# Node loop of a graph network kernel: the hidden product takes x by columns, the norm's factor goes behind it

## The chip, the cores and the metric

The kernel runs on one core of a Trainium2 chip. The metric is the device time of one execution in microseconds; beside it each profiled execution has a span, from its first to its last instruction. PE is TensorE, DVE VectorE, ACT ScalarE, POOL GpSimd, and SP the engine that issues the plain transfers.

## The reference

10,000 nodes of 512 numbers (`x`), 2,500 edges with 128 attributes each. Everything is float32.

```
h   = layernorm(x)                                   # no gain, no shift
m   = relu([h[src], attr] @ W1.T + b1) @ W2.T + b2   # per edge
agg = segment_sum(m, dst)
gi  = agg @ W_ih.T + b_ih ;  gh = h @ W_hh.T + b_hh  # 3 x 512 columns each
r, z = sigmoid(i_r + h_r), sigmoid(i_z + h_z)
n   = tanh(i_n + r * h_n)
h_new = (1 - z) * n + z * h
x1  = x + h + gamma * (h_new - run_mean) / sqrt(run_var + eps) + beta
h2  = layernorm(x1)
y   = x1 + 2 of 8 experts (512 -> 32 -> 512, chosen by a gate) of h2 + half a shared expert of h2
```

## The kernel before

Every fp32 product is made of three fp32r products: each operand is split into a high part (a rounding copy) and a low part (the rest), and hi*hi, hi*lo and lo*hi are added up in PSUM. A product of a tile of 128 rows by 512 x 512 is therefore twelve matmuls.

**Edges.** The 2,560 edges (padded) go in five super-groups of four tiles. For each the sources are gathered, normalised, turned on PE, sent through both layers, summed by destination, and multiplied by W_ih; the result, 3 x 512 columns per edge tile, is stored in a table in DRAM (`gates_in`). PE is busy nearly all of this time. In the last super-group the products with W_ih stand alone (`product`, L1146), while W_hh is loaded in four blocks of 128 x 1536 (L593, L604), ACT rounds them (`whh_hi`, L720) and DVE takes the rest (`whh_lo`, L815).

**Nodes.** Then follows a loop over 79 tiles of 128 nodes (`periods`, four tiles per loop step, the first and last ones written out). Each engine has its own body, in order, and the bodies meet through semaphores. `p.has(k)` marks what belongs to the tile k ahead of the current one. Per tile t:

- SP loads `xt` of tile t+2 (L1195) and stores the output of tile t-3 (L1185).
- DVE makes the first norm's mean and variance of tile t+2 (`first_norm`, L469, L454, L461, L462); POOL makes from it 1/sqrt (`rstd`, L1220), `shift` (L1223) and `one_rstd` (L1226).
- ACT makes `h` and `x_h` = x + h of tile t+1 (`first_rows`, L478, L481), POOL adds the batch norm's shift (`x_h_b`, L1264) and gathers the row of the edge table (`gates`, L1212).
- PE turns `h` of tile t+1 by four transposes (`turn_h`, L493), ACT rounds it from PSUM (`h_hi`, L1308), DVE takes the rest (`h_low`, L488).
- PE multiplies `h` of tile t by the three thirds of W_hh: r, n, then z (`gate`, L1455, twelve matmuls each). The z product is cut into two halves: ahead of the first comes `turn_h`, between them the transposes of `h2` of tile t-1.
- DVE adds the gates to r and z (`r_pre` L1438, `z_pre` L1384), ACT copies the n product (`hn_raw`, L1293), POOL adds the bias (`hn`, L1237), multiplies by r (`r_hn`, L1242), adds the gates (`n_pre`, L1246); ACT makes the tanh (`n_gate`, L1321), POOL h - n (`h_n`, L1251); five DVE instructions end in `x1` (L1403 to L1413).
- The second norm goes DVE, POOL (L1220, L1223), ACT (`h2`, L1298), PE (transposes), ACT (`h2_hi`, L1312), DVE (`h2_lo`, L1371), PE (twelve products with the experts' first layer, L1492).
- DVE makes `hid` (L1344 to L1365), PE turns it, ACT and DVE split it (`hid_hi` L1316, `hid_lo` L1375), PE multiplies (L1502, L1504), DVE adds `x1` into `y` (L1443).

ACT's order in a body is: `h`, `x_h`, `hn_raw`, `h2`, `r_gate`, `h_hi`, `h2_hi`, `hid_hi`, `n_gate`, `z_gate`, the experts' weights. POOL's is: second norm, `hn`, `r_hn`, `n_pre`, `h_n`, first norm, gather, `x_h_b`. DVE's is: `hid`, `first_norm`, `h2_lo`, `hid_lo`, `h_lo`, `z_pre`, the choice of experts, `x1` and its statistics, `r_pre`, `y`.

Before tile 0, DVE also splits the experts' weights (L1418 to L1431), ahead of `r_pre` of tile 0.

## Time and profile before

| what | value |
|---|---|
| three runs | 1437.27, 1438.11, 1442.31 us, median 1438.11 |
| profiled execution | 1442.45 us, of which span 1440.6 us |
| mean granted clock of TensorE | 0.989 |
| PE busy | 1378.2 us, 96% |
| PE weight loads (beside the matmuls) | 1136.4 us, 79% |
| DVE busy | 1098.6 us, 76% |
| ACT busy | 606.5 us, 42% |
| POOL busy | 900.3 us, 62% |
| memory traffic | 154.94 MB, mean 108 GB/s |

The profiled execution is 1.85 us longer than its span. A busy time counts the instructions of an engine that last; an engine that waits for a semaphore is idle. Matmuls overlap each other, and their ends are modelled, so the starts of consecutive matmuls say more than their durations. Lines such as L1455 are lines of the kernel before; helpers such as L493 serve several places, and the tile names tell them apart.

### The profile page before, as it was taken

The numbers are of one execution on the slowest core, as the hardware profiler recorded it, in microseconds if no ns is written. First come the engines' busy times: TensorE is split into PE (matmuls) and PEld (weight loads), VectorE is DVE, ScalarE is ACT, GpSimd is POOL, SyncE is SP. The second block draws the span as 40 slices with busy tenths as digits, with TensorE's granted clock in tenths as the row PEclk, the third lists the DMA queues.
The fourth block names the chain that finished last, engine by engine and source line by source line (L and its number), as shares of the span: only waits on it lengthen the run. The fifth ranks groups of instructions, "written<-read, shape, count | busy, mean of one in ns | idle before, by whom it ended". The sixth has DMA issues, their size and how long they took to land. (4 is left out here: it accounts for less than half of the span.)

```text
span 1440.6 us, 22894 instructions
## 1 busy us (share of the span) xinstructions
PE 1378.2 (96%) x6714; PEld 1136.4 (79%) x6714; DVE 1098.6 (76%) x2746; ACT 606.5 (42%) x1088; POOL 900.3 (62%) x1037
## 2 busy tenths in 40 slices
PE   4899999999899999999999999999999999999996
PEld 3678888787678888888888888888888888888884
DVE  3586334234588988888888888888888888888885
ACT  3431212202244444445444544454445444544441
POOL 3210142102387788878887788778887788778871
PEclk9999999999999999999999999999999999999997
DMA  8211432246323223322332233223322332333220
GB/s 306 68 68 64 161 129 103 88 144 223 142 95 110 99 83 109 109 92 90 109 109 89 93 109 109 84 98 109 109 81 101 109 108 76 107 109 104 79 94 30
DMA packets 50625, 154.94 MB, mean 108 GB/s; under 512 B 7840, under 2 KB 8480, under 8 KB 50464
## 3 DMA queue, kind: packets, MB, share of 16 engines
q0 software_dynamic: 15920, 79.97, 16.3%
q1 hardware_dynamic: 34672, 74.55, 14.3%
q8 instruction: 18, 0.29, 0.1%
q14 instruction: 15, 0.12, 0.0%
HBM read 117.22 MB, written 37.28 MB: 107 GB/s over the span
## 5 line engine op out<-in xcount | busy, mean ns | idle before, releaser
L1455 PE MATMUL bank<-whh_hi,h_hi 128*128 128x512 f32 x948 | 384.4, 406 | 7.0 <-DVE h_lo L488 7.0
L1455 PE MATMUL bank<-whh_hi,h_lo 128*128 128x512 f32 x948 | 373.3, 394 | 0.0
L1455 PE MATMUL bank<-whh_lo,h_hi 128*128 128x512 f32 x948 | 371.3, 392 | 0.0
L1455 PEld LDWEIGHTS bank<-whh_hi,h_hi 128*128 128x128 f32 x948 | 178.6, 188 | 41.1 <-DVE h_lo L488 7.4
L1455 PEld LDWEIGHTS bank<-whh_hi,h_lo 128*128 128x128 f32 x948 | 178.1, 188 | 39.0
L1455 PEld LDWEIGHTS bank<-whh_lo,h_hi 128*128 128x128 f32 x948 | 179.0, 189 | 34.1
L1212 POOL DMA_INDIRECT gates<-gates_in,slot_at x79 | 119.1, 1507 | 64.7 <-POOL slot_at L1210 63.3
L1293 ACT ACTIVATE hn_raw<-bank 128x512 f32<-128x512 f32 x79 | 47.2, 597 | 259.9 <-PE bank L1455 259.9
L1251 POOL TENSOR_TENSOR h_n<-h,n_gate 128x512 f32<-128x512 f32 x79 | 102.5, 1297 | 58.7 <-ACT n_gate L1321 58.7
L1237 POOL TENSOR_TENSOR hn<-hn_raw,hn_bias 128x512 f32<-128x512 f32 x79 | 104.0, 1317 | 45.5 <-ACT hn_raw L1293 45.5
L1264 POOL TENSOR_TENSOR x_h_b<-x_h,bn_shift 128x512 f32<-128x512 f32 x79 | 103.4, 1309 | 20.9 <-ACT x_h L481 18.4
L1492 PE MATMUL bank<-f_hi,h_hi 128*128 128x296 f32 x316 | 103.3, 327 | 11.3 <-DVE h_lo L1371 8.7
L1242 POOL TENSOR_TENSOR r_hn<-r_gate,hn 128x512 f32<-128x512 f32 x79 | 102.6, 1299 | 15.1 <-ACT r_gate L1303 4.1
L1246 POOL TENSOR_TENSOR n_pre<-r_hn,gates 128x512 f32<-128x512 f32 x79 | 101.0, 1279 | 12.4 <-POOL r_hn L1242 7.1
L493 PE MATMUL bank<-ident,h 128*128 128x128 f32 x632 | 95.2, 273 | 9.3 <-ACT h L1298 9.2
L493 PEld LDWEIGHTS bank<-ident,h 128*128 128x128 f32 x632 | 78.5, 141 | 31.2 <-ACT h L1298 11.0
L1146 PE MATMUL bank<-wih_hi,a_hi 128*128 128x512 f32 x240 | 95.5, 398 | 4.6 <-DVE wih_lo L815 2.5
L1220 POOL TENSOR_TENSOR rstd<-var_eps,minus_half 128x1 f32<-128x1 f32 x158 | 91.6, 580 | 9.1 <-DVE var_eps L462 9.1
L1492 PE MATMUL bank<-f_lo,h_hi 128*128 128x296 f32 x316 | 95.2, 301 | 0.0
L1492 PE MATMUL bank<-f_hi,h_lo 128*128 128x296 f32 x316 | 95.1, 301 | 0.0
L478 ACT ACTIVATE h<-xt,shift,rstd 128x512 f32<-128x512 f32 x79 | 64.5, 817 | 70.8 <-POOL one_rstd L1226 70.8
L1146 PE MATMUL bank<-wih_hi,a_lo 128*128 128x512 f32 x240 | 94.1, 392 | 0.0
(176 smaller groups left out, 3179.3 us busy)
## 6 DMA issues: line engine op xcount, KB each, us to landing
xt<-in_x SPq DMA_DIRECT2D x79, 256.0 KB, 3.1
out<-y SPq DMA_DIRECT2D x79, 256.0 KB, 3.0
gates_in<-g_out SPq DMA_DIRECT2D x16, 768.0 KB, 3.3
wih_lo_raw<-in_wih_t SPq DMA_DIRECT2D x4, 768.0 KB, 16.1
whh_lo_raw<-in_whh_t SPq DMA_DIRECT2D x4, 768.0 KB, 7.6
gates_in<-late_out SPq DMA_DIRECT2D x6, 256.0 KB, 5.7
gates_in<-g_out SPq DMA_DIRECT2D x6, 256.0 KB, 2.0
m_lo_raw<-in_attr_t SPq DMA_DIRECT2D x5, 256.0 KB, 2.7
```

What stands on the lines that cost most here:

```text
L478: act.activation(h[:, s, :], xt[:, s, :], ACT.Identity, bias=shift[1][:, s:s + 1], scale=rstd[1][:, s:s + 1]).then_inc(h_done, 1)
L493: last = pe.transpose(to[:, k * R:(k + 1) * R], rows_of[:, k * P:(k + 1) * P], ident[0:R, 0:R])
L1146: last = pe.matmul(to[0:R, :], a[:, k, j * R:(j + 1) * R], w[:, k, q * D:(q + 1) * D], start=n == 0, stop=n == 3 * DK - 1)
L1212: pool.indirect_dma_start(out=gates[:, s, :], out_offset=None, in_=gates_in, in_offset=bass.IndirectOffsetOnAxis(ap=slot_at[:, s:s + 1], a ...
L1220: pool.tensor_tensor(rstd[which][:, s:s + 1], var_eps[which][:, :], minus_half[0:R, 0:1], ALU.pow)\
L1237: pool.tensor_tensor(hn[:, s, :], hn_raw[:, s, :], hn_bias[:, :], ALU.add).then_inc(hn_done, 1)
L1242: pool.tensor_tensor(r_hn[:, :], r_gate[:, :], hn[:, s, :], ALU.mult).then_inc(r_hn_done, 1)
L1246: pool.tensor_tensor(n_pre[:, :], r_hn[:, :], gates[:, s, 2 * D:G3], ALU.add).then_inc(n_pre_done, 1)
L1251: pool.tensor_tensor(h_n[:, :], h[:, s, :], n_gate[:, s, :], ALU.subtract).then_inc(h_n_done, 1)
L1264: pool.tensor_tensor(x_h_b[:, s, :], x_h[:, s, :], bn_shift[:, :], ALU.add).then_inc(x_h_b_done, 1)
L1455: last = pe.matmul(to[0:R, :], a[:, s, k * R:(k + 1) * R], w[:, k, q * D:(q + 1) * D], start=n == 0, stop=n == 3 * DK - 1)
L1492: last = pe.matmul(b_f1[0:R, 0:F1], a[:, k * R:(k + 1) * R], w[:, k, :], start=n == 0, stop=n == 3 * DK - 1)
```

## The change

A second input is added, `x_cols`: for each node tile the same numbers of x, arranged by the host with the 512 features on the partitions. The product takes x instead of h. As h = rstd * (x - mean), and the mean of a row times the column sums of W_hh is what x @ W has too much, the rows of W_hh are centred on the chip: from each of the 1,536 rows its mean over the 512 inputs is subtracted, which makes the product of x equal to that of x - mean. The factor rstd multiplies the product where it leaves PSUM.

- Gone: the four transposes of `h` per tile, `h_hi`, `h_lo` and one PSUM bank's use for them. The bank serves as a second one for the r product, so that the wait for `r_pre` is one tile looser.
- Per tile new: SP's load of 256 KB of `x_cols` into the memory of `x_lo`, behind a wait for the z product; ACT's `x_high`, DVE's `x_low`, now from SBUF.
- `r_pre` and `z_pre` become scalar_tensor_tensor with `rstd`, `hn_raw` becomes an Identity with a scale.
- `first_norm` moves from DVE (four instructions) to ACT (four other ones), behind `x_h` and ahead of `hn_raw`.
- During the edges: four loads of three rows per partition of W_hh, twelve ACT instructions that sum them, a store of the means and their broadcast (768 KB); after the edges' last gathers POOL subtracts them in four instructions of 128 x 1536, and ACT's rounding waits for it.
- The experts' split on DVE moves from ahead of `r_pre` of tile 0 to behind its `z_pre`, two of its six steps are merged away; ACT's part of it moves behind `r_gate`.

```diff
-    def first_norm(dve, p):
-        s = p.slot(2)
-        dve.wait_ge(x_in[s], 16 * (p.turn(2) + 1))
-        dve.bn_stats(st[1][:, :], xt[:, s, :]).then_inc(st_done[1], 1)
-        statistics(dve, p, 2, 1)
-        mean_var(dve, p, 2, 1)
+    ROOT = math.sqrt(D)
+    def first_norm(act, p):
+        t, s = p.t, p.slot(2)
+        act.wait_ge(x_in[s], 16 * (p.turn(2) + 1))
+        wait_from(act, shift_done[1], 2 * (t + 2))
+        act.activation(squares[:, :], xt[:, s, :], ACT.Copy, scale=-1.0 / D, accum_out=neg_mean[1][:, :])\
+            .then_inc(mv_done[1], 1)
+        act.wait_ge(mv_done[1], t + 3)
+        act.activation(root_mean[:, :], neg_mean[1][:, :], ACT.Copy, scale=1.0 / ROOT).then_inc(root_done, 1)
+        act.wait_ge(root_done, t + 3)
+        act.activation(squares[:, :], xt[:, s, :], ACT.Square, bias=root_mean[:, :], scale=1.0 / ROOT,
+                       accum_out=var1[:, :]).then_inc(st_done[1], 1)
+        act.wait_ge(st_done[1], t + 3)
+        act.activation(var_eps[1][:, :], var1[:, :], ACT.Identity, bias=eps_col[:, :]).then_inc(var_done[1], 1)
...
-    def h_low(dve, p):
+    def x_high(act, p):
         s = p.slot(1)
-        dve.wait_ge(h_hi_done, p.t + 2)
-        dve.tensor_tensor(h_lo[:, s, :], b_th[:, 0:DK * R], h_hi[:, s, :].bitcast(F32), ALU.subtract)\
-            .then_inc(h_lo_done, 1)
+        act.wait_ge(cols_in[s], 16 * (p.turn(1) + 1))
+        wait_from(act, z_prod, p.t)
+        act.activation(x_hi[:, s, :], x_raw[:, s, :], ACT.Copy).then_inc(x_hi_done, 1)
+
+    def x_low(dve, p):
+        s = p.slot(1)
+        dve.wait_ge(x_hi_done, p.t + 2)
+        dve.tensor_tensor(x_lo[:, s, :], x_raw[:, s, :], x_hi[:, s, :].bitcast(F32), ALU.subtract)\
+            .then_inc(x_lo_done, 1)
...
@@ after the carries of the last super-group, POOL
+            pool.wait_ge(mean_back, 16)
+            for k in range(DK):
+                pool.wait_ge(whh_in[k], 16)
+                pool.tensor_tensor(whh_raw[:, k, :], whh_raw[:, k, :], whh_mean[:, :], ALU.subtract)\
+                    .then_inc(whh_centred, 1)
...
+            def sums_of_whh(n):
+                act.wait_ge(rows_in, 16 * (n + 1))
+                for i in range(3):
+                    at = 3 * n + i
+                    act.activation(whh_rows[:, i, :], whh_rows[:, i, :], ACT.Copy, scale=1.0 / D,
+                                   accum_out=mean_cols[:, at:at + 1]).then_inc(rows_summed, 1)
...
@@ ACT ahead of the node loop
             for k in range(DK):
+                if k == 0:
+                    first_norm(act, Period(0, -FIRST - 2))
                 if k == 2:
-                    first_rows(act, Period(0, -FIRST - 1))
-                act.wait_ge(whh_in[k], 16)
+                    first_norm(act, Period(0, -FIRST - 1))
+                    for j in range(2):
+                        x_high(act, Period(0, j - FIRST - 1))
+                act.wait_ge(whh_centred, k + 1)
                 hi_of(whh_hi[:, k, :], whh_raw[:, k, :]).then_inc(whh_hi_done, 1)
+            first_rows(act, Period(0, -FIRST - 1))
...
@@ SP's body of the node loop
                 if p.has(-3):
                     store(t - 3, p.slot(-3))
+                if p.has(2) and not p.early(2):
+                    wait_from(sp, z_prod, t + 1)
+                    sp.dma_start(x_raw[:, s, :], x_cols[bass.ds(at, 1), :, :].rearrange("o p r -> p (o r)"))\
+                        .then_inc(cols_in[s], 16)
...
@@ ACT's body
+                if p.has(2) and not p.early(2):
+                    first_norm(act, p)
                 if p.has(0):
                     act.wait_ge(n_prod, t + 1)
                     wait_from(act, hn_done, t - 1)
-                    act.activation(hn_raw[:, s, :], b_n[0:R, :], ACT.Copy).then_inc(hn_raw_done, 1)
+                    act.wait_ge(rstd_done[1], t + 1)
+                    act.activation(hn_raw[:, s, :], b_n[0:R, :], ACT.Identity,
+                                   scale=rstd[1][:, p.slot4(0):p.slot4(0) + 1]).then_inc(hn_raw_done, 1)
...
-                if p.has(1):
-                    act.wait_ge(h_turned, t + 2)
-                    wait_from(act, z_prod, t)
-                    act.activation(h_hi[:, s, :], b_th[:, 0:DK * R], ACT.Copy).then_inc(h_hi_done, 1)
+                if p.has(1) and not p.early(1):
+                    x_high(act, p)
...
@@ DVE's body
-                if p.has(2) and not p.early(2):
-                    first_norm(dve, p)
...
-                if p.has(1) and not p.first(1):
-                    h_low(dve, p)
+                if p.has(1) and not p.early(1):
+                    x_low(dve, p)
...
-                    dve.tensor_tensor(z_pre[:, :], b_z[0:R, :], gates[:, s, D:2 * D], ALU.add)
+                    dve.scalar_tensor_tensor(z_pre[:, :], b_z[0:R, :], rstd[1][:, p.slot4(0):p.slot4(0) + 1],
+                                             gates[:, s, D:2 * D], ALU.mult, ALU.add)
+                if p.first(0):
+                    split_of_experts(dve)
...
@@ PE's body
-                    pe.wait_ge(h_lo_done, t + 1)
-                    wait_from(pe, r_pre_done, t)
-                    gate(s, b_r, 0).then_inc(r_prod, 1)
+                    pe.wait_ge(x_lo_done, t + 1)
+                    wait_from(pe, r_pre_done, t - 1)
+                    gate(s, b_r[s], 0).then_inc(r_prod, 1)
                     wait_from(pe, hn_raw_done, t)
                     gate(s, b_n, 2).then_inc(n_prod, 1)
-                if p.has(1) and not p.first(1):
-                    turn_h(pe, p)
```

## Rows read from the trace of the kernel before

**Rows 1.** Windows: stretch, length, busy time of each engine, clock, DMA share, GB/s.
```profile
423.31:1395.84 972.53, 962.24 (x4886) 799.55 (x4885) 862.27 (x2296) 475.70 (x888) 778.19 (x889) 1.00 0.29 100
```
**Rows 2.** Timeline of ACT: start, duration, instruction, [idle before, what ended it].
```profile
423.31 0.60 ACT L1293 ACTIVATE hn_raw<-bank 128x512 f32<-128x512 f32 x1 [3.06 <-PE bank L1455]
...
1395.84 0.60 ACT L1293 ACTIVATE hn_raw<-bank 128x512 f32<-128x512 f32 x1 [3.18 <-PE bank L1455]
```
**Rows 3.** Timeline of PE in the tile at 900 us, and the next.
```profile
900.65 0.41 PE L1492 MATMUL bank<-f_hi,h_hi 128*128 128x296 f32 x1
...
909.47 0.60 PE L493 MATMUL bank<-ident,h 128*128 128x128 f32 x4
909.83 0.48 PE L1455 MATMUL bank<-whh_hi,h_hi 128*128 128x512 f32 x1
910.14 0.40 PE L1455 MATMUL bank<-whh_lo,h_hi 128*128 128x512 f32 x1
...
911.30 0.60 PE L493 MATMUL bank<-ident,h 128*128 128x128 f32 x4
...
913.13 0.49 PE L493 MATMUL bank<-ident,hid 128*128 128x128 f32 x3
```
**Rows 4.** Groups by line, weight loads, 423.31 to 1395.84: busy, mean ns, idle before.
```profile
L1492 PEld LDWEIGHTS bank<-f_hi,h_hi 128*128 128x128 f32 x296 | 55.7, 188 | 27.8 <-DVE h_lo L1371 27.8
```
**Rows 5.** Groups by line, POOL, the same stretch.
```profile
L1237 POOL TENSOR_TENSOR hn<-hn_raw,hn_bias 128x512 f32<-128x512 f32 x74 | 96.8, 1308 | 42.4 <-ACT hn_raw L1293 42.4
```
**Rows 6.** Timeline of ACT in the tile at 909 us.
```profile
909.75 0.60 ACT L1293 ACTIVATE hn_raw<-bank 128x512 f32<-128x512 f32 x1 [3.32 <-PE bank L1455]
910.24 0.81 ACT L1298 ACTIVATE h<-x,shift,rstd 128x512 f32<-128x512 f32 x1
...
911.95 0.59 ACT L1312 ACTIVATE h_hi<-bank 128x512 fp32r<-128x512 f32 x1
```
**Rows 7.** Groups by line and shape, ACT, the whole span.
```profile
L743 ACT ACTIVATE r_lo_raw<-bank,b_col 128x512 f32<-128x512 f32 x20 | 13.7, 687 | 39.6 <-PE bank L1098 39.6
L720 ACT ACTIVATE r_hi<-r_lo_raw 128x512 fp32r<-128x512 f32 x20 | 12.6, 632 | 0.6
...
L1303 ACT ACT_TABLE_LOAD x1 | 1.3, 1283 | 0.0
```
**Rows 8.** Timelines of POOL and PE in the tile at 410 us.
```profile
410.75 0.40 POOL L1223 TENSOR_TENSOR shift<-neg_mean,rstd 128x1 f32<-128x1 f32 x1
...
412.05 0.65 PE L493 MATMUL bank<-ident,h 128*128 128x128 f32 x4 [1.17 <-ACT h L1298]
```
**Rows 9.** Timelines of POOL and DVE, tiles at 425, 900 and 910 us.
```profile
425.56 0.20 DVE L1365 TENSOR_TENSOR hid<-extra,hid 128x41 f32<-128x41 f32 x1
...
900.26 1.28 POOL L1246 TENSOR_TENSOR n_pre<-r_hn,gates 128x512 f32<-128x512 f32 x1 [0.17 <-POOL r_hn L1242]
901.14 0.42 DVE L1375 TENSOR_TENSOR hid_lo<-bank,hid_hi 128x256 fp32r<-128x256 f32 x1 [0.54 <-ACT hid_hi L1316]
902.28 1.30 POOL L1251 TENSOR_TENSOR h_n<-h,n_gate 128x512 f32<-128x512 f32 x1 [0.74 <-ACT n_gate L1321]
...
910.51 1.36 POOL L1237 TENSOR_TENSOR hn<-hn_raw,hn_bias 128x512 f32<-128x512 f32 x1 [0.65 <-ACT hn_raw L1293]
910.75 1.18 DVE L1365 TENSOR_TENSOR hid<-extra,hid 128x41 f32<-128x41 f32 x1
```
**Rows 10.** Timelines of ACT, DVE and PE between edges and nodes.
```profile
355.68 1.49 ACT L720 ACTIVATE whh_hi<-whh_lo_raw 128x1536 fp32r<-128x1536 f32 x1 [0.39 <-DMA whh_lo_raw<-in_whh_t]
...
373.11 0.39 PE L1455 MATMUL bank<-whh_hi,h_hi 128*128 128x512 f32 x1
...
386.29 0.68 DVE L1438 TENSOR_TENSOR r_pre<-bank,gates 128x512 f32<-128x512 f32 x1
...
399.40 0.66 PE L493 MATMUL bank<-ident,h 128*128 128x128 f32 x4 [1.61 <-ACT h L1298]
```
**Rows 11.** The page, DMA issues: transfer, queue, count, size, median us to landing.
```profile
xt<-in_x SPq DMA_DIRECT2D x79, 256.0 KB, 3.1
```

More of the change, by code:

```diff
@@ L86, in gnn_ffn @@
     iota8 = place("iota8", [R, NE])
+    eps_col = place("eps_col", [R, 1])
     node_slot = place("node_slot", [R, NT], I32)
@@ L302, in gnn_ffn @@
     x_h_b = place("x_h_b", [R, 2, D])
[L303 to L306 removed]
+    x_hi = place("x_hi", [P, 2, DK * R], F32R)
+    x_lo, x_raw = place_low("x_lo", [P, 2, DK * R])
+    st = {2: place("st2", [R, 6])}
+    mv = {2: place("mv2", [R, 2])}
     var_eps = {k: place(f"var_eps{k}", [R, 1]) for k in (1, 2)}
     neg_mean = {k: place(f"neg_mean{k}", [R, 1]) for k in (1, 2)}
[L309 removed]
+    squares = place("squares", [R, D])
+    root_mean = place("root_mean", [R, 1])
+    var1 = place("var1", [R, 1])
+    rstd = {1: place("rstd1", [R, UNROLL]), 2: place("rstd2", [R, 2])}
     shift = {k: place(f"shift{k}", [R, 2]) for k in (1, 2)}
@@ L574, in _ @@
                 for j in range(1, SUP):
+                    if j == 2 and g > 1:
+                        rows_of_whh(2 * g - 3)
                     store(SUP * (g - 1) + j)
+                if g == 1:
+                    sp.wait_ge(bias_stored, 16)
+                if g < NSUP - 2:
+                    rows_of_whh(2 * g - 2)
                 if g == 2:
@@ L593, in _ @@
                 sp.dma_start(whh_raw[:, k, :], whhv[:, k, :]).then_inc(whh_in[k], 16)
+            for t in range(2):
+                sp.dma_start(x_raw[:, t, :], x_cols[t, :, :]).then_inc(cols_in[t], 16)
             for j in range(2, SUP):
@@ L1059, in _ @@
             last = EC - SUP
-            for k in range(2):
-                whh_lo_of(k)
-            for j in range(2):
-                for q in range(3):
-                    take_gates(last + j, q)
-            take_gates(last + 2, 0)
-            whh_lo_of(2)
-            take_gates(last + 2, 1)
-            whh_lo_of(3)
-            take_gates(last + 2, 2)
-            h_low(dve, Period(0, -FIRST - 1))
+            for q in range(3):
+                take_gates(last, q)
+            for q in range(3):
+                take_gates(last + 1, q)
+                if q < 2:
+                    whh_lo_of(q)
+            for j in range(2):
+                x_low(dve, Period(0, j - FIRST - 1))
+            for q in range(3):
+                take_gates(last + 2, q)
+                if q > 0:
+                    whh_lo_of(q + 1)
             for q in range(3):
@@ L1172, in _ @@
                 sums(g)
-            for j in range(SUP - 1):
+            for j in range(SUP):
                 product(NSUP - 1, j)
-            turn_h(pe, Period(0, -FIRST - 1))
-            product(NSUP - 1, SUP - 1)
             pe.wait_ge(g_added, 3 * EC - 3)
@@ L1453, in gate @@
                 for k in range(k0, k1):
-                    for a, w in ((h_hi, whh_hi), (h_hi, whh_lo), (h_lo, whh_hi)):
+                    for a, w in ((x_hi, whh_hi), (x_hi, whh_lo), (x_lo, whh_hi)):
                         last = pe.matmul(to[0:R, :], a[:, s, k * R:(k + 1) * R], w[:, k, q * D:(q + 1) * D],
```

118 lines of the change are left out of this document (67 added, 51 removed).

## Prediction

> **What bounds the kernel now.** I read the windows first: of a span of 1440.6 us the stretch from the fourth node tile to the 78th takes 972.5 us, with TensorE (PE) busy 962.2 us at clock 1.00 [rows 1], so the node loop and PE in it decide. Its period comes from the timeline of ACT: hn_raw starts 74 periods apart at 423.31 and 1395.84 us [rows 2], 13.142 us each; with one period of the same loop before and one behind I count 76. The reader is to see three things in it.
>
> PE is in order and nearly full. Its one stall is ahead of the first expert product (L1492), which waits for DVE's low half of the second norm: 27.8 us over 74 tiles, 0.376 us each [rows 4]; its length is the idle time of the weight loads, as the matmuls' ends are modelled.
>
> POOL (GpSimd) comes close behind. It waits for hn_raw 42.4 us over 74 tiles, 0.573 us each [rows 5]. Without that wait its own sequence, with its round trips to ACT, needs 13.142 - 0.573 = 12.57 us.
>
> A chain runs through both. POOL's second-norm shift of a tile goes to ACT (h2), to PE's transposes of h2, through eleven more microseconds of PE to the next hn_raw, and back to POOL.
>
> **What the change takes from PE.** The four transposes of h go. They begin at 909.47, the next product begins at 909.83, and the one behind it 0.31 us later, where products of 512 columns otherwise follow each other every 0.23 us [rows 3]: 0.36 + 0.08 = 0.44 us. With the stall gone too, PE would need 13.142 - 0.44 - 0.376 = 12.33 us. That isn't reached, for what was hidden behind 0.44 us of transposes appears.
>
> **What is late next: h2.** On ACT h2 (L1298) stands behind hn_raw, and both behind the end of the hn product. From where the next product would issue (909.47), hn_raw starts 0.28 later and h2 ends at 911.05, 1.58 later [rows 3, 6]; PE could transpose some 0.06 later, at 1.64. PE now gets there after transposes and six products; without the transposes after 6 x 0.23 = 1.38. So PE stalls 0.25 us. hn_raw also becomes an Identity with a scale read from SBUF. The rows have 0.632 us for a copy of 512 columns without such an operand and 0.687 from PSUM with one; hn_raw, a copy from PSUM, takes 0.60, so one costs about 0.09, and h with two takes 0.81 [rows 6, 7]. I take +0.10 (bounds 0 and 0.2).
>
> After h2's transposes comes h2_hi. x_high takes the place of h_hi between r_gate and h2_hi, 0.63 us from SBUF [rows 7]. h2_hi started 0.65 us after the transposes' start (911.30 to 911.95) [rows 6]; with h2 tight ahead, ACT is free for it only at about 0.89. Then 0.59 for it, 0.68 for h2_lo (a DVE instruction on 512 columns, such as r_pre [rows 10]) and 0.12 for two hand-overs put the expert product at 2.28 us, where PE arrives at 1.83 + 0.29 = 2.12: a stall of 0.16. DVE is free for it, since first_norm's four instructions, one of them on 512 columns, are taken away ahead of it. PE's own loop is 12.33 + 0.25 + 0.10 + 0.16 = 12.84 us.
>
> **The loop over two periods.** In the tile at 410.75 the shift ends at 411.15 and PE transposes at 412.05: 0.90 us [rows 8]. From there PE needs 1.83 to hid's transposes (911.30 to 913.13), 0.29 for them at 0.09 each, the stall of 0.16, and from the first expert product to the end of hn's products 8.82 (900.65 to 909.47) [rows 3]: 11.10. Then 0.28 to hn_raw, 0.70 for it and 0.16 to POOL: 13.14 in all. POOL needs 12.57 to the shift of that tile. (13.14 + 12.57) / 2 = 12.86 us, which I take for the period. The saving is 13.142 - 12.86 = 0.28 us; times 76, **-21.5 us**.
>
> **ACT's new work** is four instructions a tile: two of 512 columns and two of one column, each waiting for the one before. They stand behind x_h and ahead of hn_raw, and ACT idles 3.32 us there [rows 6]. Nothing in the rows accumulates along a row. Lower bound: 0.63 + 0.2 + 0.7 + 0.2 = 1.7 us by [rows 7], with 0.2 for a short one as the engine's overhead (0.63 less the share of the columns). Upper: 0.82 for each long one, and for every accumulator result a further short instruction and four waits as long as POOL's 0.17 [rows 9]: 3.3 us. I take 2.5, the middle. The gap becomes 3.32 - 0.3 = 3.0 us, so it costs nothing, with 0.5 us to spare; beyond 3.0 us each further 0.1 us adds about 0.1 us to the period (+7.6 us).
>
> The tile of x it reads: SP issues that load now behind the column load, which waits for the z product, about 9.2 us into PE's period. Two transfers of 256 KB, of which one lands in 3.1 us [rows 11], take 3.5 to 4.5 us and are there 1 to 2 us before ACT reads. The column tile is read by ACT only behind r_gate, another 5 us later. What is queued behind SP's new wait is this x load and the output store of an older tile, which has a whole period. The traffic rises from 100 to about 120 GB/s; I charge nothing (bound +3 us).
>
> **DVE.** r_pre and z_pre get a scale; I charge 0 (bounds 0 and +0.1 us each, the price of such an operand on ACT; off the path either way, for DVE is busy 862 of 972 us [rows 1] and loses first_norm). x_low replaces h_low at some 0.69 us as before, but reads two SBUF tiles where h_low read PSUM and one. What the trace shows of that: hid's last step (two SBUF inputs, 41 columns) takes 0.20 us alone, but 1.18 us when it is started behind POOL's hn, and ends 0.06 us after hn does [rows 9]. So x_low may be held up by POOL, or hold it up. It comes behind hid_lo, whose end (901.56) falls at n_pre's end (901.54); the next POOL instruction waits 0.74 us for n_gate [rows 9], and x_low fits. I take 0; bounds: -0.1 (DVE's other work comes earlier) and +0.69 us a period, if it gets between two POOL instructions that would follow each other at once.
> The Trainium skill, "SBUF — State Buffer", in "SBUF: two separate sides", says that VectorE with two SBUF inputs and a GpSimd instruction that reads SBUF hold their common port pair for the whole instruction, so that the other waits in full. The trace agrees (1.18 against 0.20 us). By this rule the change carries a price that its instruction count does not show: the sum would be +0.69 x 76 = +52 us on POOL's part if x_low always took the pair ahead of a ready instruction, and 0 in the gap.
>
> **Ahead of the node loop.** W_hh's row sums are twelve ACT instructions in two super-groups of edges, where ACT is mostly idle: 0 (bound +2 us). POOL centres four blocks of 128x1536. At 1.3 to 1.36 us for 512 columns [rows 9] each takes 3.8 us; the last two blocks land late (whh_hi of the last starts at 355.68, behind its transfer) [rows 10], and two centrings of them behind each other end at about 361.5; then the norm of tile 0 and 2.2 us of tile 1's, two x_high, two whh_hi and two low halves: about 372, just as PE comes to the node loop (373.11 [rows 10], less 0.36). I take 0; bounds -0.4 and +8 us, if each block costs 5 us beside DVE. In return r_pre of tile 0 no longer stands behind the experts' split (386.29) [rows 10]; but the split then stands ahead of tile 0's z_h_n, and h2 of tile 0, for which PE waits at 399.40 [rows 10], comes at the same time within 1 us by the order of the code. PE does tile 1's r earlier and waits longer there. So 0, bounds -3 and +3.
>
> **Sum.** The profiled run took 1442.45 us (span 1440.6 and 1.85 around it); 1442.45 - 21.5 = 1420.9. The median of before is 1438.11, 4.3 us below it, so I state 1416.6 against that median: 1416.6 / 1438.11 = 0.985.
>
> **Rivals.**
> 1. POOL alone bounds, 12.57 us: h2 and hn_raw come sooner than worked out. For it: in the tile at 410.75 POOL is already what PE waits for, 1.17 us [rows 8]. Against: h2's place behind hn_raw. 76 x 0.57 = -43: 1395.
> 2. x_low and POOL meet, in part: some 0.3 us of POOL's cycle. (13.14 + 12.87) / 2 = 13.0, -11: 1427.
> 3. Slower: x_low gets in front of n_pre. Its place is the 0.15 us between r_hn and n_pre; it decides once hid_lo ends before r_hn does. POOL then needs 12.57 + 0.69 = 13.26, or +0.12 x 76 = +9: 1447. For it: hid's 41 columns slip in just so. Against: hid_lo ends at 901.56, r_hn at 900.09 in the tile shown [rows 9].
> 4. Square and Sigmoid do not share a function table: two loads a tile. A load lasts 1.28 us, and there is one for all of the node loop [rows 7]; 2.5 + 2.56 in a gap of 3.0 is +2.06 a tile above 12.86: 1573. The Trainium skill, "ScalarE: Activation LUTs", in "Table sets: the hidden batching unit", has the cheap functions in every set and loads only at a switch, which speaks against this one; no run here has a Square yet.
> 5. ACT's gap of 3.0 is too small for 3.3 us of work: 12.86 + 0.3 = 13.16: no change, 1439.
>
> **Chances.** Forecast 0.48, rival 1 0.18, rival 2 0.14, rival 3 0.08, rival 4 0.03, rival 5 0.05, the rest (0.04) centring that costs 8 us, 1425. A measurement of this kernel can tell about 0.5%, 7 us, from no change. Faster: 0.46 of the forecast, rival 1, 0.10 of rival 2 and the rest: 0.78; same: 0.02, 0.04 and 0.04 of rival 5: 0.10; slower: rivals 3 and 4 and 0.01 of rival 5: 0.12. The range leaves out rivals 3 and 4 and half of 1: 1398 to 1440.
>
> **What would show it.** Period from hn_raw starts: 12.86; 13.1 or more refutes it, 12.6 is rival 1. Right: a PE stall of 0.2 to 0.4 us ahead of h2's transposes with ACT h2 as releaser, ACT's first_norm within 2.5 us and idle left ahead of hn_raw, POOL's wait for hn_raw down from 0.57 to 0.3. x_low near 0.7 us: no meeting; 1 us or more: rival 2. Table loads more than two: rival 4.

## The result, and the profile after

The changed kernel takes 1445.9 us, the median of five runs (1442.4 to 1448.2); the kernel before took 1438.1 beside it. The ratio is 1.005, 95% interval 1.003 to 1.007: a little slower. 1416.6 was forecast, with a range to 1440.

The profiled execution has a span of 1445.1 us, 4.5 more than before. From [rows 2] and the two starts of hn_raw below (timeline of ACT: start, duration, instruction, idle before and what ended it), the 75 periods from tile 3 on take 987.78 us, or 13.170 each. Before they took 13.137 each (the last hn_raw started at 1408.55): 75 x 0.033 = +2.5. The measured loop starts 3.45 us later (426.76 against 423.31) and the end behind it is 1.5 shorter. Sum 4.5. The loop's forecast was 12.86.

```profile
426.76 0.69 ACT L1363 ACTIVATE hn_raw<-bank,rstd 128x512 f32<-128x512 f32 x1 [2.82 <-PE bank L1528]
...
1414.54 0.69 ACT L1363 ACTIVATE hn_raw<-bank,rstd 128x512 f32<-128x512 f32 x1 [4.92 <-PE bank L1528]
```

The windows view answers to [rows 1]: PE is 13 us less busy in a stretch that is 3 us shorter, DVE 26 less, ACT 145 more.

```profile
426.76:1396.00 969.24, 948.90 (x4565) 758.52 (x4564) 836.41 (x1983) 620.48 (x1324) 767.23 (x881) 1.00 0.36 119
```

**Two kinds of tiles.** The mean hides the point. I paired each start of POOL's hn with the three steps of DVE's `hid` beside it (from tile 3 to 1400 us). A step is called held up when it starts while an instruction of POOL runs and lasts until that one is over. Before, the first step starts 0.10 to 0.46 us ahead of hn in all 74 periods, and one of the three steps is held up by hn. After, that is so in most, and 48 of 73 periods take 12.92 us on average, near the forecast. In 25 the first step starts 0.00 to 0.13 us *behind* hn, two steps are held up, and these take 13.67. This is the pair at 901 and 914 us, DVE first:

```profile
901.62 0.42 DVE L1443 SCALAR_TENSOR_TENSOR hid<-f,extra 128x256 f32<-128x256 f32 x1
901.97 1.30 DVE L1448 CAST hid<-extra 128x82 fp32r<-128x82 f32 x1
903.30 0.20 DVE L1451 TENSOR_TENSOR hid<-extra,hid 128x41 f32<-128x41 f32 x1
...
914.95 1.45 DVE L1443 SCALAR_TENSOR_TENSOR hid<-f,extra 128x256 f32<-128x256 f32 x1
916.32 1.29 DVE L1448 CAST hid<-extra 128x82 fp32r<-128x82 f32 x1
917.65 0.20 DVE L1451 TENSOR_TENSOR hid<-extra,hid 128x41 f32<-128x41 f32 x1
917.77 0.68 DVE L1455 TENSOR_TENSOR h_lo<-bank,h_hi 128x512 fp32r<-128x512 f32 x1
```

POOL beside it:

```profile
901.75 1.45 POOL L1307 TENSOR_TENSOR hn<-hn_raw,hn_bias 128x512 f32<-128x512 f32 x1 [0.32 <-ACT hn_raw L1363]
903.34 1.31 POOL L1312 TENSOR_TENSOR r_hn<-r_gate,hn 128x512 f32<-128x512 f32 x1
...
914.83 1.29 POOL L1307 TENSOR_TENSOR hn<-hn_raw,hn_bias 128x512 f32<-128x512 f32 x1 [0.40 <-ACT hn_raw L1363]
916.26 1.29 POOL L1312 TENSOR_TENSOR r_hn<-r_gate,hn 128x512 f32<-128x512 f32 x1
```

In the first tile `hid`'s 0.42 us step is ahead of hn by 0.13 us and runs; the CAST behind it is held until hn is over, and the last step runs in the gap before r_hn. In the second hn is ahead by 0.12: the first step takes 1.45 us, the CAST comes just as r_hn has begun and takes 1.29. hid is ready 3.0 us after hn's start, not 1.75. PE, forecast to be past this point, waits (timeline of PE; line 525 serves both transposes):

```profile
915.43 0.66 PE L525 MATMUL bank<-ident,h 128*128 128x128 f32 x4 [0.22 <-ACT h L1369]
...
917.98 0.54 PE L525 MATMUL bank<-ident,hid 128*128 128x128 f32 x3 [0.49 <-DVE hid L1451]
```

The groups by line, stretch 430 to 1396 us (busy, mean ns, idle before), show it as means, beside the other terms of the forecast. The names of tiles come without their numbers: the h_lo that the experts' product waits for, here and in all later rows, is `h2_lo`, and the h that the transposes of L525 wait for is `h2`.

```profile
L1448 DVE CAST hid<-extra 128x82 fp32r<-128x82 f32 x73 | 74.5, 1020 | 0.0
L520 DVE TENSOR_TENSOR x_lo<-x_lo_raw,x_hi 128x512 fp32r<-128x512 f32 x74 | 59.1, 799 | 0.0
L1443 DVE SCALAR_TENSOR_TENSOR hid<-f,extra 128x256 f32<-128x256 f32 x73 | 57.7, 791 | 0.7
L1510 DVE SCALAR_TENSOR_TENSOR r_pre<-bank,rstd,gates 128x512 f32<-128x512 f32 x73 | 54.8, 751 | 0.2
...
L1307 POOL TENSOR_TENSOR hn<-hn_raw,hn_bias 128x512 f32<-128x512 f32 x73 | 98.3, 1347 | 50.4 <-ACT hn_raw L1363 49.5
...
L1363 ACT ACTIVATE hn_raw<-bank,rstd 128x512 f32<-128x512 f32 x73 | 50.4, 690 | 85.3 <-PE bank L1528 85.3
...
L1563 PEld LDWEIGHTS bank<-f_hi,h_hi 128*128 128x128 f32 x296 | 55.8, 189 | 12.0 <-DVE h_lo L1455 7.2
L525 PEld LDWEIGHTS bank<-ident,h 128*128 128x128 f32 x292 | 30.6, 140 | 41.7 <-ACT h L1369 41.7
```

### The profile page after: what moved, and what is told of

It reads as the page before. It is cut to its first block and busy times, and to the rows that moved or that the text cites. A ratio compares the mean times of both kernels' runs of the same rounds, so it can differ in the third digit from the quotient of the medians.

```text
span 1445.1 us, 22692 instructions
## 1 busy us (share of the span) xinstructions
PE 1367.7 (95%) x6398; PEld 1096.4 (76%) x6398; DVE 1076.2 (74%) x2428; ACT 772.1 (53%) x1586; POOL 909.6 (63%) x1042
## 5 line engine op out<-in xcount | busy, mean ns | idle before, releaser
L1528 PE MATMUL bank<-whh_hi,x_hi 128*128 128x512 f32 x948 | 381.6, 402 | 0.8 <-DVE whh_lo L883 0.7
L1528 PE MATMUL bank<-whh_hi,x_lo 128*128 128x512 f32 x948 | 375.1, 396 | 0.0
L1528 PE MATMUL bank<-whh_lo,x_hi 128*128 128x512 f32 x948 | 374.8, 395 | 0.0
L1528 PEld LDWEIGHTS bank<-whh_hi,x_lo 128*128 128x128 f32 x948 | 178.3, 188 | 42.9
L1528 PEld LDWEIGHTS bank<-whh_hi,x_hi 128*128 128x128 f32 x948 | 178.5, 188 | 40.4 <-issue 1.1
L1528 PEld LDWEIGHTS bank<-whh_lo,x_hi 128*128 128x128 f32 x948 | 178.6, 188 | 39.8
L1322 POOL TENSOR_TENSOR h_n<-h,n_gate 128x512 f32<-128x512 f32 x79 | 109.1, 1381 | 60.0 <-ACT n_gate L1394 60.0
L1363 ACT ACTIVATE hn_raw<-bank,rstd 128x512 f32<-128x512 f32 x79 | 54.5, 690 | 96.9 <-PE bank L1528 96.9
L1213 PE MATMUL bank<-wih_lo,a_hi 128*128 128x512 f32 x240 | 93.5, 390 | 0.0
L1389 ACT ACTIVATE hid_hi<-bank 128x384 fp32r<-128x384 f32 x79 | 38.9, 492 | 94.3 <-PE bank L525 94.2
```

The lines of the kernel that those rows point to most:

```text
L1213: last = pe.matmul(to[0:R, :], a[:, k, j * R:(j + 1) * R], w[:, k, q * D:(q + 1) * D], start=n == 0, stop=n == 3 * DK - 1)
L1322: pool.tensor_tensor(h_n[:, :], h[:, s, :], n_gate[:, s, :], ALU.subtract).then_inc(h_n_done, 1)
L1363: act.activation(hn_raw[:, s, :], b_n[0:R, :], ACT.Identity, scale=rstd[1][:, p.slot4(0):p.slot4(0) + 1]).then_inc(hn_raw_done, 1)
L1528: last = pe.matmul(to[0:R, :], a[:, s, k * R:(k + 1) * R], w[:, k, q * D:(q + 1) * D], start=n == 0, stop=n == 3 * DK - 1)
```

## The experiments

Theory 1 after the result: DVE's sequence, with its meetings with POOL, paced the loop before; the change freed PE, which did not pace it. Rivals: ACT's new norm is at fault, or PE's new stall ahead of h2. Each ratio is against the kernel before, measured beside that run (medians 1438.1 to 1440.3); periods are means of the starts of POOL's r_hn, of 75 intervals (74 with the norm back on DVE).

| run | first_norm | y | product of | hn, r_gate | period | time, us | ratio, 95% |
|---|---|---|---|---|---|---|---|
| before | DVE | old | h | POOL | 13.137 | 1438.1 | |
| e3 | DVE | old | h, one transpose | POOL | 13.078 | 1437.9 | 0.996 to 0.998 |
| e4 | DVE | old, made twice | h | POOL | 15.04 | 1586.6 | 1.099 to 1.103 |
| e5 | ACT | old | h | POOL | 13.084 | 1442.2 | 1.001 to 1.003 |
| e11 | ACT, its load left on DVE | old | h | POOL | 13.159 | 1445.2 | 1.003 to 1.006 |
| e7 | DVE | old | x | POOL | 13.306 | 1456.9 | 1.010 to 1.013 |
| after | ACT | old | x | POOL | 13.170 | 1445.9 | 1.003 to 1.007 |
| e2 | DVE | late | h | POOL | 13.203 | 1443.1 | 1.002 to 1.004 |
| e6 | ACT | late | h | POOL | 12.814 | 1419.9 | 0.984 to 0.987 |
| e1 | ACT | late | x | POOL | 12.931 | 1425.8 | 0.988 to 0.991 |
| e8 | ACT | late | x | DVE | 12.808 | 1417.2 | 0.983 to 0.986 |
| e10 | ACT | late | h | DVE, r first | 12.708 | 1409.0 | 0.977 to 0.981 |
| e9 | ACT | late | x | DVE, r first | 12.664 | 1405.9 | 0.975 to 0.978 |
| e12 | ACT | late | x | DVE, hn ahead of `hid` | 12.945 | 1425.5 | 0.989 to 0.992 |

**Where a period goes.** These are means over the 72 to 74 tiles between 430 and 1396 us, from the starts and ends in the timelines, in us. Each row begins where the one above it ends.

| from, to | before | e3 | e7 | e5 | after | e1 |
|---|---|---|---|---|---|---|
| hn_raw's start, hn's start | 0.696 | 0.697 | 0.786 | 0.694 | 0.787 | 0.788 |
| hn's start, its end | 1.306 | 1.290 | 1.289 | 1.320 | 1.347 | 1.294 |
| hn's end, `hid`'s end | 0.105 | 0.059 | 0.069 | 0.956 | 0.772 | -1.053 |
| `hid`'s end, h2_lo's start | 1.223 | 1.226 | 1.243 | 0.309 | 0.336 | 1.964 |
| h2_lo's start, the experts' first matmul | 0.736 | 0.737 | 0.735 | 0.771 | 0.743 | 0.746 |
| that matmul, the next hn_raw's start | 9.066 | 9.068 | 9.190 | 9.041 | 9.192 | 9.193 |
| sum | 13.132 | 13.076 | 13.312 | 13.091 | 13.177 | 12.930 |

In after and e1, h2_lo waits for h2_hi in the undisturbed tiles (29.3 and 103.8 us of idle time ahead of it, over 74 and 75), so there the rows say where the time lies and not what sets it. In the kernel before every handover in this ring is at once, so it is the ring that sets the period: the end of the n product starts hn_raw and hn, hn holds `hid`'s last step, DVE goes on with `first_norm` and h2_lo in its order, PE's experts' product waits for that, and the next n product ends nine microseconds later. One turn of it, from the timelines of DVE, PE and ACT (hn_raw at 909.75 and hn at 910.51 are in [rows 6] and [rows 9]):

```profile
911.86 0.68 DVE L469 BATCH_NORM_STATS2 st<-xt 128x6 f32<-128x512 f32 x1
...
913.15 0.68 DVE L1371 TENSOR_TENSOR h_lo<-bank,h_hi 128x512 fp32r<-128x512 f32 x1
...
913.88 0.41 PE L1492 MATMUL bank<-f_hi,h_hi 128*128 128x296 f32 x1 [0.27 <-DVE h_lo L1371]
...
922.95 0.60 ACT L1293 ACTIVATE hn_raw<-bank 128x512 f32<-128x512 f32 x1 [3.41 <-PE bank L1455]
```

The transposes of `h` are not in this ring: PE makes them between the n product and the wait for h2_lo, beside hn and `first_norm`.

**PE's pace by columns.** The last row but one of the table grows by 0.12 with the product of x. Its matmuls follow each other more slowly, though the granted clock is 1.00 in both stretches: 23 intervals take 5.36 us here and 5.26 before (timelines of PE, after, then before).

```profile
908.06 0.39 PE L1528 MATMUL bank<-whh_hi,x_hi 128*128 128x512 f32 x1
...
913.42 0.39 PE L1528 MATMUL bank<-whh_hi,x_lo 128*128 128x512 f32 x1
```

```profile
917.26 0.39 PE L1455 MATMUL bank<-whh_hi,h_hi 128*128 128x512 f32 x1
...
922.52 0.39 PE L1455 MATMUL bank<-whh_hi,h_lo 128*128 128x512 f32 x1
```

The mean interval in this stretch, longer gaps left out, is 0.233 us in all six kernels that multiply x and 0.228 to 0.229 in all eight that multiply h. Over 36 matmuls that is 0.17 us a tile, of the 0.44 that the transposes were to give. Why it is so was not tested.

**e1, after with y late.** `y` (0.68 us) stands ahead of `hid` on DVE; here it goes behind `hid` of the next body.

```diff
@@ DVE's body, behind hid
+                if p.has(-3):
+                    s = p.slot(-3)
+                    dve.wait_ge(f2_prod, t - 2)
+                    wait_from(dve, y_stored[s], 16 * p.turn(-3))
+                    dve.tensor_tensor(y[:, s, :], b_f2[0:R, :], x1[:, p.slot4(-3), :], ALU.add).then_inc(y_done, 1)
```

> The changed kernel, with DVE's y of a tile moved behind the next body's hid, so that hid's steps start some 0.6 us earlier against POOL's hn. Theory 1 (meeting of DVE and POOL): in the changed kernel every third tile hid's first step with two SBUF inputs starts behind hn and is held up twice, hid ends 2.8 to 3.0 us behind hn's start instead of 1.4 to 1.8, PE waits, and the tile takes 13.7 instead of 12.85 us. With hid 0.6 us earlier this is gone: period 12.85 to 12.9 throughout, 75 x 0.3 = 22 us less than the changed kernel, 1421 to 1427. Theory 2 (the ring of POOL, h2 and PE is longer on average than I worked out, hid is a symptom): within 5 us of the changed kernel, 1441 to 1449. Theory 3 (the column transfers or x_low from SBUF slow the loop): the same 1441 to 1449, with tiles of 13.7 left.

1425.8 us. `hid` now starts at least 0.54 us ahead of hn in every period, and no period has two held steps. The 25 tiles of 13.67 are gone, and 12.93 is 0.07 above the forecast. So the forecast's loop through POOL, h2 and PE is near once DVE is out of its way: PE waits 43.9 us over 74 tiles for h2, and DVE itself idles 103.8 over 75 (groups of e1, DVE):

```profile
L1460 DVE TENSOR_TENSOR h_lo<-bank,h_hi 128x512 fp32r<-128x512 f32 x75 | 51.9, 692 | 103.8 <-ACT h_hi L1385 103.8
```

**e2, before with y late.** The same edit in the kernel before.

> The kernel before, with only DVE's y moved behind the next body's hid. In its tiles hid's last step is held up once by hn (1.18 instead of 0.20 us). Theory 1: hid is done before hn starts, DVE gains 1 us ahead of first_norm and h2_lo, and PE's stall of 0.376 us ahead of the experts' product shrinks to under 0.1: period 12.8 to 12.9, 20 to 26 us less, 1412 to 1420. Theory 2 and 3: DVE isn't what the stall waits for (h2_hi ends just ahead of h2_lo anyway): within 5 us of before.

1443.1, against the expectation. y had moved ahead of first_norm and h2_lo, that is, into the ring of the table: PE waits 31.3 us over 73 tiles for h_lo, most of it in every other tile. In e1 the room behind `hid` had been made by first_norm's leaving.

**e3, before with one of four transposes of h.** Three of `turn_h`'s four are left out.

```diff
-        turn(pe, b_th, h[:, p.slot(1), :], DK).then_inc(h_turned, 1)
+        turn(pe, b_th, h[:, p.slot(1), :], 1).then_inc(h_turned, 1)
```

> The kernel before, with one transpose of h a tile instead of four: three of four blocks of h's columns are left out. Nothing else of the change is in it: first_norm on DVE, h_low from PSUM, no new transfer. PE has 0.27 us a tile less. Theory 1: the shorter period alone brings hn nearer to the end of POOL's sequence and hid behind its start, so that tiles of 13.5 us and more appear and the gain is under half of 0.27 x 76 = 20 us: 1428 to 1441. Theory 3 (x_low, the transfers, ACT's norm): none of them is here, so the whole 20 us are gained: 1415 to 1421.

1437.9, ratio 0.996 to 0.998: 0.06 us a tile of the 0.33 taken from PE. The number lies in theory 1's range, but its reason does not show: every tile has one held step, as before, and none has two. The freed time turned into waits of PE: for h2_lo 37.3 us over 73 tiles, where [rows 4] had 27.8 over 74, and for h2, for which it had not waited in this stretch, 17.6. In the table below the runs, its column is nearly that of before. The prediction's reading that PE's own time decides fails here by itself.

**e4, before with one more DVE instruction** of 0.75 us ahead of `hid` (a second y into a spare tile).

```diff
+                    dve.tensor_tensor(spare_y[:, :], b_f2[0:R, :], x1[:, p.slot4(-2), :], ALU.add).then_inc(spare_done, 1)
+                    dve.wait_ge(spare_done, t - 1)
```

> The kernel before, with one more DVE instruction of y's form (PSUM and one SBUF input, written to a tile that nobody reads) ahead of hid: hid starts some 0.75 us later against hn. DVE is idle 11% of the loop. Theory 1: hid's first step now starts behind hn in most tiles and is held up twice; the period grows by 0.4 to 0.8 us, 1468 to 1500. Theory 2 and 3: DVE has the room, within 10 us of before.

1586.6, ratio 1.099 to 1.103: 1.9 us a tile, far beyond both theories, and not by the mechanism that was expected, for one tile of 75 has two held steps and 71 have one. In the terms of the table, `hid` ends 1.39 us behind hn instead of 0.11, and the way from the experts' first matmul to the next hn_raw takes 9.64 us instead of 9.07. The second part is the clock: PE waits 1.2 us a tile for h2_lo here, and the granted clock, 1.00 in the loop before, falls to its lower level (1.2 GHz) again and again (windows view of e4):

```profile
441.00:1553.00 1112.00, 1014.67 (x4882) 833.27 (x4881) 968.44 (x2365) 468.50 (x886) 717.63 (x882) 0.96 0.26 86
```

So 0.57 of the 1.9 us is no price of DVE's time. The periods vary from 12.5 to 18.0 us, which was not followed. The run shows that time on DVE ahead of `hid` is not free, and gives no price for it.

**e5, before with only first_norm on ACT.** The change's ACT instructions, nothing else of it.

> The kernel before with only one part of the change: first_norm is made by ACT (its four instructions) and not by DVE. The product still takes h by four transposes. Theory A (before is bound by DVE's sequence, whose last meeting point is PE's wait for h_lo ahead of the experts' product, 0.376 us): DVE loses some 1.3 us a tile ahead of h2_lo, the wait of 0.376 goes, and the period falls from 13.14 towards PE's own 12.77; allowing for a part of the tiles in which hid is held up by hn twice, 12.8 to 13.0 us, or 1412 to 1430 us in all. Theory B (the ACT norm itself is what made the changed kernel slow, by ACT's order or by DVE's hid moving against POOL's hn): PE's wait moves from the experts' product to hid's transposes, period 13.15 or more, 1440 us or more.

1442.2, ratio 1.001 to 1.003: neither theory's number. DVE is relieved and PE's wait for h_lo falls to 9.5 us over 73 tiles, as expected. But this wait had kept hn late. Two consecutive tiles, timeline of DVE:

```profile
492.01 1.51 DVE L1377 SCALAR_TENSOR_TENSOR hid<-f,extra 128x256 f32<-128x256 f32 x1
493.44 1.30 DVE L1382 CAST hid<-extra 128x82 fp32r<-128x82 f32 x1
...
505.13 0.42 DVE L1377 SCALAR_TENSOR_TENSOR hid<-f,extra 128x256 f32<-128x256 f32 x1
505.47 1.29 DVE L1382 CAST hid<-extra 128x82 fp32r<-128x82 f32 x1
```

and the timeline of POOL beside it:

```profile
491.94 1.30 POOL L1255 TENSOR_TENSOR hn<-hn_raw,hn_bias 128x512 f32<-128x512 f32 x1 [0.31 <-ACT hn_raw L1313]
...
505.38 1.33 POOL L1255 TENSOR_TENSOR hn<-hn_raw,hn_bias 128x512 f32<-128x512 f32 x1 [1.18 <-ACT hn_raw L1313]
```

`hid` 0.07 behind hn: two held steps. 0.25 ahead: one. 37 periods with two held steps take 13.40, 37 others 12.78. Half the tiles gain 0.36, half lose 0.26. The r_hn of tile 3 comes at 428.27, after 425.61 before. This delay is there from tile 0 on (390.44, 387.71 before), where the changed kernel is ahead (385.47), so it does not explain the later start of that one.

**e11, the same with DVE's load given back:** four instructions of first_norm's kinds, on a constant tile, at its old place; nothing uses their result.

```diff
+                    dve.bn_stats(st_idle[:, :], bn_scale[:, :]).then_inc(idle_done, 1)
+                    dve.wait_ge(idle_done, 2 * (t - 1) - 1).then_inc(held["dve"], 1)
+                    dve.bn_aggr(mv_idle[:, :], st_idle[:, :]).then_inc(idle_done, 1)
+                    dve.wait_ge(idle_done, 2 * (t - 1))
+                    dve.tensor_scalar(out_idle[:, 0:1], mv_idle[:, 0:1], -1.0, None, ALU.mult)
+                    dve.tensor_scalar(out_idle[:, 1:2], mv_idle[:, 1:2], EPS, None, ALU.add)
```

> The kernel before with first_norm on ACT, and on DVE, at first_norm's old place, four instructions of the same kinds and lengths whose result nothing uses. It tells whether it is the relief of DVE or the new work on ACT that makes tiles of 12.7 and 13.4 us alternate. Theory A (DVE's relief: PE's wait for h_lo, which kept hn late, is gone, and hn gets in front of hid): with the load back PE waits 0.3 to 0.4 us for h_lo again, hid starts 0.3 to 0.5 us ahead of hn in every tile, one step of it is held up, no tile is longer than 13.5, the period is 13.1 to 13.2. Theory B (ACT's new work): the alternation stays, and with DVE's load on top the period is 13.3 or more, 1452 us or more.

1445.2, period 13.159. No period has two held steps; `hid` starts 0.08 to 0.46 ahead of hn in all 73, as before, and PE waits for h_lo again (groups, weight loads):

```profile
L1520 PEld LDWEIGHTS bank<-f_hi,h_hi 128*128 128x128 f32 x295 | 55.6, 189 | 29.5 <-DVE h_lo L1399 29.5
```

So it was the relief of DVE that brought the double meetings, not ACT's work. The wait that the prediction counted as a gain was what kept hn behind `hid`.

**e6, e5 with y late.**

> As the run with only first_norm on ACT, and y of a tile made one body later, behind hid, so that hid's first step starts ahead of hn. The four transposes stay. Theory A (transposes cost nothing while DVE bounds, and DVE's load and the phase of hid against hn decide): no tile with two held-up steps, period 12.80 to 12.95, 1412 to 1426 us, that is within 0.5% of the changed kernel with the same shift of y (1425.8). Theory B (the products by columns are worth their 0.44 us a tile once DVE is out of the way): it stays above 12.93 + 0.2, 1440 us or more.

1419.9: theory A. With its transposes, and without the column input, it is 5.9 us faster than e1, although it has one held step in nearly every tile (`hid`'s last one, 1244 ns) and e1 hardly any. It lacks hn_raw's scale and the slower products (9.06 us in the table's last row but one, 9.19 in e1). PE's wait for h2 is 12.8 us over 75 tiles where e1 had 43.9 over 74. The transposes fill the time in which h2 is made.

**e7, after with first_norm back on DVE.**

> The changed kernel with first_norm put back on DVE (bn_stats, two short instructions and the aggregate), behind hid; ACT loses its four. Theory A (DVE's sequence sets the period): DVE now carries r_pre, z_pre with their scale, x_low and first_norm, about 1.3 us more than in the changed kernel and some 0.2 us more than before: 13.3 us or more a tile, 1455 to 1500 us. Theory B (the norm on ACT is at fault): at or below the changed kernel, 1420 to 1446 us.

1456.9: theory A's number, but not by its reason. No period has two held steps, and it is still 0.17 us a tile above before. r_pre takes 751 ns (683 before), z_pre 739 (680), x_lo 765 (h_lo 680): 0.21 us more on DVE. Yet the table's rows on DVE's part are as before (`hid`'s end to h2_lo 1.243 and 1.223). What grows is the way to hn by 0.09, which is hn_raw's scale, and PE's way from the experts to hn_raw by 0.12. PE waits for h2_lo as before:

```profile
L511 DVE TENSOR_TENSOR x_lo<-x_lo_raw,x_hi 128x512 fp32r<-128x512 f32 x73 | 55.8, 765 | 0.0
...
L1553 PEld LDWEIGHTS bank<-f_hi,h_hi 128*128 128x128 f32 x292 | 55.1, 189 | 38.3 <-DVE h_lo L1445 38.2
```

**e8, e1 with hn made by DVE** in one instruction from PSUM; ACT's hn_raw and POOL's hn are gone.

```diff
+                    dve.scalar_tensor_tensor(hn[:, s, :], b_n[0:R, :], rstd[1][:, p.slot4(0):p.slot4(0) + 1],
+                                             hn_bias[:, :], ALU.mult, ALU.add).then_inc(hn_done, 1)
```

> The changed kernel with y of a tile behind the next body's hid, and hn made by one DVE instruction from PSUM (product * rstd + bias), placed behind hid; ACT's hn_raw and POOL's hn are gone. Theory A (the meetings of DVE's hid with POOL's hn are what is paid, about 1.2 us of DVE's time a tile): the new instruction of some 0.75 us costs less than the hold-up of 1.2 us, h2 on ACT stands behind nothing, and the period comes to 12.4 to 12.6 us, 1385 to 1402 us. Theory B (DVE is simply short of time by instruction lengths): 0.75 us more on DVE makes it 13.1 or more, 1440 us or more.

1417.2, between the theories. It is 8.6 us faster than e1, but misses the range of theory A by 15. POOL now waits for r_gate, which stands on ACT behind h2, and h2 waits for POOL (groups, POOL):

```profile
L1310 POOL TENSOR_TENSOR r_hn<-r_gate,hn 128x512 f32<-128x512 f32 x75 | 97.0, 1294 | 111.8 <-ACT r_gate L1368 109.7 <-DVE hn L1452 2.1
```

**e9, e8 with r_gate ahead of h2 on ACT.**

> The run with hn on DVE, in which POOL waits 1.46 us a tile for r_gate because that stands on ACT behind h2, which waits for POOL's shift. Here ACT makes r_gate ahead of h2. Theory A (this loop through ACT's order bounds at 12.81): POOL waits only for hn now, some 0.9 us, and its loop falls by 0.5 us to 12.3; PE takes over with 12.33 and a stall ahead of h2's transposes: 12.35 to 12.55 us a tile, 1380 to 1397 us. Theory B (PE, with its stall ahead of h2's transposes, already bounds): 12.75 to 12.85, 1412 to 1420 us.

1405.9, ratio 0.977 [0.975, 0.978]: the fastest, 40 us below the changed kernel and 34 below the kernel before as measured beside it. It misses the range of theory A by 9 us: POOL waits for hn, which DVE makes behind `hid`, 121.7 us over 75 tiles, and PE still waits 33.0 over 76 for h2.

**e10, e9 with the product of h,** transposes included.

> Everything of the run with hn on DVE and r_gate ahead of h2, but without the change's product: the kernel before takes h by four transposes, DVE adds the plain n product and the bias in one instruction, first_norm is on ACT and y stands behind hid. It measures what the input by columns is worth once DVE and POOL are out of the way. Theory A (PE bounds, and the transposes are then on the path): PE's own 12.77 and up to 0.1 of stalls, 12.77 to 12.90 us, 1410 to 1424 us, that is 20 to 35 us above the same kernel by columns. Theory B (the transposes still fill a wait for h2): the two are within 7 us of each other.

1409.0. The two ratios' intervals overlap; columns are worth 3 us, 0.044 a tile (theory B). PE's wait for h2 is 7.1 us over 76 tiles here and 33.0 by columns. Without it the periods are 12.61 and 12.23: PE did lose time by columns, 0.38 us a tile, the slower products counted in, and got most of it back as a wait.

**e12, e9 with hn ahead of `hid`'s steps on DVE,** so that POOL gets it sooner.

> The run with hn on DVE and r_gate ahead of h2, where POOL waits 1.6 us a tile for hn, because DVE makes it behind the three steps of hid, although the n product ends some 0.5 us before. Here hn stands on DVE ahead of hid's three steps; PE turns hid some 1.5 us after hid is ready there, so hid may come 0.7 us later. Theory A (POOL's sequence, started by hn, ends in the shift for which h2 and PE's stall of 0.43 us wait): hn and all behind it come 0.4 to 0.5 us sooner, the stall shrinks, the period falls from 12.66 to 12.40 to 12.52 us, 1384 to 1396 us. Theory B (hid, or h2_lo behind it, becomes late for PE): 12.66 or more, 1404 us or more.

1425.5, ratio 0.989 to 0.992, period 12.945 in every tile (12.91 to 12.96): theory B, 20 us slower than e9. hn came earlier, but r_hn with it, and now `hid`'s CAST meets r_hn each time (timeline of DVE):

```profile
915.10 0.75 DVE L1440 SCALAR_TENSOR_TENSOR hn<-bank,rstd,hn_bias 128x512 f32<-128x512 f32 x1 [0.29 <-PE bank L1534]
915.77 0.41 DVE L1446 SCALAR_TENSOR_TENSOR hid<-f,extra 128x256 f32<-128x256 f32 x1
916.10 1.28 DVE L1451 CAST hid<-extra 128x82 fp32r<-128x82 f32 x1
```

POOL beside it:

```profile
916.00 1.32 POOL L1310 TENSOR_TENSOR r_hn<-r_gate,hn 128x512 f32<-128x512 f32 x1 [1.64 <-DVE hn L1440]
```

DVE is 1.1 us later for it and PE waits 36.1 us over 74 tiles for h_lo. I had again forecast an order and left out the meeting that it makes.

## Why the prediction was wrong

**The step that failed** is the one from PE's waits to the period: "PE is in order and nearly full", its stall of 0.376 us [rows 4] and its 0.44 us of transposes taken off as gains, and the meetings of DVE and POOL at `hid` left out of the sum. Two things were wrong in it.

First, PE's time did not decide. A stall that ends with DVE's h2_lo in every tile was the sign of a ring through ACT, POOL and DVE that comes back to PE there; I read it as a remainder to be collected. The transposes lie beside the ring. e3 shows it (PE's time taken away: 0.06 us of 0.33), and so does e6, which keeps them and is faster than e1. What did open the ring was first_norm's leaving DVE: 0.89 us between `hid` and h2_lo in the table.

Second, **the price of a meeting was looked for at the wrong place.** The prediction had the 1.18 us of `hid`'s last step behind hn [rows 9] and asked only whether the new x_low would meet POOL. Rival 2 did so too. What moved was hn itself against the old `hid`: with the ring shorter it came from 0.10 to 0.46 behind `hid`'s start to as much as 0.13 ahead in a third of the tiles. 25 periods with 0.75 us more are 18.7 us, and 75 x (13.170 - 12.86) = 23 us are to be explained in the loop; the rest is the 0.06 by which the other tiles exceed 12.86. In the table the way from hn's end to `hid`'s end grows by 0.67, against the 0.89 gained. e1 takes the second held step away and has 12.93 throughout; e5 and e11 show that the relief of DVE brings it.

The charge of 0 for the scale of r_pre and z_pre, "off the path either way, for DVE is busy 862 of 972 us [rows 1] and loses first_norm", had a weak reason, for a busy share of 89% says nothing of the order; but e7 shows no loss in DVE's part of the ring. Whether r_pre's 0.07 us decides which tiles have `hid` behind hn is not shown.

The Trainium skill, "SBUF — State Buffer", in "SBUF: two separate sides", says that the engine that starts first keeps the pair for the whole instruction and the other waits in full. The pairs at 901 and 914 us agree: DVE's step 0.13 us ahead and the step takes 0.42 us, 0.12 us behind and it takes 1.45. The prediction cited this rule for a place that the edit touches, and not for the places whose order in time it shifts.

**Steps that held.** The period of the undisturbed tiles: 12.92 (12.86 forecast), and e1 12.93 throughout. The products' slower pace is a term that the sum lacked: six and 24 matmuls in its loop over two periods are 0.14 us, which makes 12.93 of 12.86, by my estimate. first_norm on ACT takes 2.1 us (897.77 to 899.89; 2.5 forecast) in its gap, and 85.3/73 = 1.15 us stay idle ahead of hn_raw. The scale operand: hn_raw 0.60 to 0.69 us (+0.10 forecast). The experts' product waits 12.0/74 = 0.16 us (0.16 forecast), disturbed tiles counted in, so the agreement is in part luck. The transfers land in 2.8 and 2.6 us. The node loop has one table load, as before, so rival 4 is out.

**Sizes that were off.** PE's wait ahead of h2 is 41.7/73 = 0.57 us; 0.35 was forecast in its two parts, since in the tiles behind a disturbed one POOL's shift is later too. POOL's wait for hn_raw rose from 0.57 to 49.5/73 = 0.68, and 0.3 was forecast. x_low takes 0.80 us where 0.69 was forecast, r_pre and z_pre 0.07 and 0.06 more each.

**The start** was put at 0. PE comes to the node products at 371.25 (373.11 before), so neither the centring nor the sums cost anything; yet the first tile measured in the loop is 3.45 us later. Up to the r_hn of tile 2 the changed kernel is ahead (412.33 against 412.59). Two held steps come in that tile (1.49 and 1.29 us at 412.46), and PE waits for hid. Behind that wait the granted clock falls to its lower level for part of 412 to 424 us (timeline of PE after; windows before, then after):

```profile
415.45 0.55 PE L525 MATMUL bank<-ident,hid 128*128 128x128 f32 x3 [1.60 <-DVE hid L1451]
```

```profile
412.00:424.00 12.00, 11.95 (x62) 10.16 (x63) 10.39 (x30) 5.76 (x12) 9.63 (x13) 1.00 0.16 47
```

```profile
412.00:424.00 12.00, 10.35 (x46) 8.45 (x45) 10.03 (x21) 6.65 (x16) 7.32 (x10) 0.86 0.24 67
```

From the experts' first matmul to tile 3's first product PE needs 4.91 us (416.05 to 420.96), 3.37 on average in the loop. So the wait of 1.60 and 1.5 of lower clock are most of the 3.45 us. e1 and e7 have the same two held steps there, a clock of 0.86 and 0.72 in this stretch, and their r_hn of tile 3 at 428.90 and 429.63. In e8 and e9, without the meetings, the clock is 1.00 there, the r_hn is at 425.13 and 425.65, and the loss is gone.

**What stays open.** Why the tiles by columns come in a pattern of two and three rather than one of two, as in e5, was not followed. Nor was the cause of the slower products by columns. That a version of the change exists in which all of its PE time would pay was not shown; in the best one tried, PE still waits 0.43 us a tile for h2.
